# Moving the queries' relu from GpSimd to VectorE, and GpSimd's waits onto its edge columns

## The reference, cut to what matters

```python
x = x + window_mixing(group_norm(x))
x = x + linear_attention(group_norm(x))     # the second stage, below

qkv  = einsum('bchw,oc->bohw', x, w_qkv)            # 768 channels: queries, keys, values
y    = conv5x5_depthwise(qkv); y = conv1x1_grouped(y)
mqkv = concat([qkv, y], axis=1)                     # heads of 8 channels for each of q, k, v
q = relu(mqkv queries); k = relu(mqkv keys); v = mqkv values, with a row of ones
vk  = einsum('bhdn,bhen->bhde', v, k)
out = einsum('bhde,bhen->bhdn', vk, q)
out = out[:, :, :-1] / (out[:, :, -1:] + eps)
out = batch_norm(einsum('bchw,oc->bohw', out, w_proj))
```

## Time and profile before

| | |
|---|---|
| time, median of 3 runs | 2473.91 us (2470.03 to 2474.42) |
| profiled execution, span | 2473.8 us |
| busy in the span: PE, DVE, ACT, POOL | 95%, 81%, 60%, 44% |
| mean granted TensorE clock | 0.987 of full speed |
| DMA over the span | 628.38 MB, 254 GB/s |

### The profile page before, as it was taken

The page is one execution under the profiler, slowest core; times in us unless marked ns, Lnnn a source line. Parts: engine busy times, 40 slices in busy tenths (PEclk is TensorE's granted clock), DMA queues, the critical chain, the costliest instruction groups (busy, mean ns, idle before and its releaser), DMA issues. The chain is left out here.

```text
span 2473.8 us, 66794 instructions
## 1 busy us (share of the span) xinstructions
PE 2359.6 (95%) x25485; PEld 1881.3 (76%) x25485; DVE 1994.9 (81%) x2653; ACT 1495.6 (60%) x1864; POOL 1099.8 (44%) x1476
## 2 busy tenths in 40 slices
PE   5999799999999999799999999999999889999998
PEld 5889688877777887577888888888888656666666
DVE  7887688878788877778888888888888588888775
ACT  5777566666566666566776776677767434433442
POOL 7722387887787878200000000000000068888887
PEclk9999899999999999899999999999999999999999
DMA  7874689988988989988888888888888777777774
GB/s 285 336 301 173 208 295 344 329 293 314 316 288 323 344 299 302 253 196 207 209 209 208 209 210 207 210 208 209 207 208 210 228 243 280 275 275 271 271 272 136
DMA packets 300973, 628.38 MB, mean 254 GB/s; under 512 B 50784, under 2 KB 252256, under 8 KB 291552
## 3 DMA queue, kind: packets, MB, share of 16 engines
q1 hardware_dynamic: 295072, 590.38, 77.5%
q10 hardware_dynamic: 4688, 31.63, 3.6%
q0 software_dynamic: 1008, 3.67, 0.4%
HBM read 327.81 MB, written 300.94 MB: 254 GB/s over the span
## 5 line engine op out<-in xcount | busy, mean ns | idle before, releaser
L1562 PE MATMUL c_ps<-dh,wh 128*128 128x512 f32 x1152 | 465.3, 404 | 15.8 <-DVE wl L1712 9.9
L1477 ACT ACTIVATE dh<-image 128x1632 fp32r<-128x1632 f32 x192 | 301.5, 1570 | 269.9 <-PE c_ps L1562 254.8
L1562 PE MATMUL c_ps<-dh,wl 128*128 128x512 f32 x1152 | 456.4, 396 | 0.0
L1562 PE MATMUL c_ps<-dl,wh 128*128 128x512 f32 x1152 | 454.6, 395 | 1.6 <-issue 1.6
L1921 POOL TENSOR_TENSOR ql<-image,qh 128x1024 fp32r<-128x1024 f32 x1 | 2.4, 2359 | 967.8 <-DVE ql L2152 967.8
L1670 DVE TENSOR_TENSOR dl<-image,dh 128x1632 fp32r<-128x1632 f32 x192 | 356.3, 1856 | 73.9 <-ACT dh L1477 73.9
L1132 PE MATMUL o_ps<-xh,wqh 128*128 128x512 f32 x768 | 319.2, 416 | 11.3 <-issue 8.4
L1909 POOL TENSOR_TENSOR ql<-image,qh 128x1024 fp32r<-128x1024 f32 x126 | 300.9, 2413 | 10.7 <-ACT qh L1940 10.7
L1132 PE MATMUL o_ps<-xl,wqh 128*128 128x512 f32 x768 | 303.5, 395 | 0.0
L1132 PE MATMUL o_ps<-xh,wql 128*128 128x512 f32 x768 | 301.9, 393 | 0.0
L1562 PEld LDWEIGHTS c_ps<-dh,wh 128*128 128x128 f32 x1152 | 218.5, 190 | 68.6 <-DVE wl L1712 10.0
(11 more groups left out here) (212 smaller groups left out, 5107.8 us busy)
## 6 DMA issues: line engine op xcount, KB each, us to landing
qkv_scratch<-stage SPq DMA_DIRECT2D x384, 408.0 KB, 4.7
image<-qkv_scratch SPq DMA_DIRECT2D x189, 816.0 KB, 6.3
yq_scratch<-qy SPq DMA_DIRECT2D x64, 512.0 KB, 6.7
image<-qr_scratch SPq DMA_DIRECT2D x128, 256.0 KB, 6.1
image<-yq_scratch SPq DMA_DIRECT2D x128, 256.0 KB, 5.3
ox<-x_scratch SPq DMA_DIRECT2D x8, 4096.0 KB, 15.3
qr_scratch<-qs SPq DMA_DIRECT2D x126, 256.0 KB, 3.6
out<-ox SPq DMA_DIRECT2D x7, 4096.0 KB, 12.7
```

Of the source, the lines that this page charges most:

```text
L1477: act.activation(dh[kind][:, :], raw[kind], ACT.Copy).then_inc(hi_ready, 1)
L1562: last = pe.matmul(c_ps[:, m, :], w[hp][:, kind, part, o:o + P], cells[:, :, HALF * dy:HALF * dy + HALF * NB], start=(k == 0), stop=(k == 5))
```

## The change

The relu of the queries goes from GpSimd to VectorE, as one instruction of 128x1024 per chunk from `qw` to `qs`, behind VectorE's two differences of the queries. VectorE then also has the wait for the store of the `qs` buffer's former content. GpSimd's `pause` is gone, and its edge columns carry the waits; the edge columns become two-input instructions, with a tile of zeros as the other input (`0 - x` and `x + 0`). The border row is zeroed behind the first edge column of its chunk instead of ahead of it, and in those chunks the wait for the stored queries stands ahead of the keys' edge column.

```diff
+            pool.memset(zero[:, :], 0.0).then_inc(zeroed, 1)
             pool.memset(vT[:, :, :, :, SQ:VS], 1.0).then_inc(zeroed, 1)
+            pool.wait_ge(zeroed, 2)
+            none = zero[:, :].unsqueeze(1).unsqueeze(2).broadcast_to([P, 4, NB, 1])
...
-                    def pause(k, n):
-
-                        k = NCH * k + n
-                        pool.tensor_tensor(tick[:, k:k + 1], K["ident"][:, 0:1], K["ident"][:, 1:2], ALU.add)
-
                     def border(n):
 
                         row = NB * (1 - n // 4)
-                        keys_values_free(pool, b, n)
-                        queries_free(pool, b, n)
-                        pause(0, n)
...
                         if n % 2:
-                            pool.tensor_scalar(staged(j0, n, 0, 0, 1), every_second(buf, t0, n, 0, 1), -1.0, None, ALU.mult)
+                            pool.tensor_tensor(staged(j0, n, 0, 0, 1), none, every_second(buf, t0, n, 0, 1), ALU.subtract)
                         else:
-                            pool.tensor_copy(staged(j0, n, 1, HALF - 1, HALF), every_second(buf, t0, n, NB - 1, 1))
+                            pool.tensor_tensor(staged(j0, n, 1, HALF - 1, HALF), every_second(buf, t0, n, NB - 1, 1), none, ALU.add)
...
                         keys_values_free(pool, b, n)
-                        pause(1 + u, n)
+                        if u == 0 and n % 4 < 2:
+                            queries_free(pool, b, n)
                         edge(kv, 2 * u, 2 * u, n)
+                        if u == 0 and n % 4 < 2:
+                            border(n)
...
                         queries_free(pool, b, n)
-                        at_least(pool, K["qr_stored"][n % 2], 32 * (4 * b + n // 2))
-                        pause(3, n)
                         edge(qw, 0, 4, n)
                         pool.tensor_copy(staged(4, n, 2), every_second(qw, 0, n, 1 - n % 2)).then_inc(q_odd, 1)
-                        if end:
-                            return
-                        for t in range(2):
-                            last = pool.tensor_scalar(qs[:, n % 2, t, :], qw[:, n % 2, t, :], 0.0, None, ALU.max)
-                        last.then_inc(qs_ready, 1)
...
-                    def queries(n):
+                    def queries(n, end=False):
...
                         differences(qw, 0, 4, n, q_diff)
+                        if end:
+                            return
+                        at_least(dve, K["qr_stored"][n % 2], 32 * (4 * b + n // 2))
+                        dve.tensor_scalar(qs[:, n % 2, :, :], qw[:, n % 2, :, :], 0.0, None, ALU.max).then_inc(qs_ready, 1)
```

More of the change, by code:

```diff
@@ L767, in projections @@
         vT = sb("vT", [P, 2, 4, NSQ, VS])
-        tick = sb("ptick", [P, 4 * NCH])
+        zero = sb("zero", [P, 1])
         pw_rep = sb("pw_rep", [P, QT, NPH, D])
@@ L922, in keys_values, with queries @@
                         keys_values_free(pool, b, n)
-                        pause(1 + u, n)
+                        if u == 0 and n % 4 < 2:
+                            queries_free(pool, b, n)
                         edge(kv, 2 * u, 2 * u, n)
+                        if u == 0 and n % 4 < 2:
+                            border(n)
                         pool.tensor_copy(staged(2 * u, n, 2), every_second(kv, 2 * u, n, 1 - n % 2)).then_inc(kv_odd, 1)
-                    def queries(n, end=False):
+                    def queries(n):
                         g = NCH * b + n
@@ L931, in queries @@
                         queries_free(pool, b, n)
-                        at_least(pool, K["qr_stored"][n % 2], 32 * (4 * b + n // 2))
-                        pause(3, n)
                         edge(qw, 0, 4, n)
                         pool.tensor_copy(staged(4, n, 2), every_second(qw, 0, n, 1 - n % 2)).then_inc(q_odd, 1)
-                        if end:
-                            return
-                        for t in range(2):
-                            last = pool.tensor_scalar(qs[:, n % 2, t, :], qw[:, n % 2, t, :], 0.0, None, ALU.max)
-                        last.then_inc(qs_ready, 1)
                     for n in range(NCH):
-                        if n % 4 < 2:
-                            border(n)
                         keys_values(n, 0)
@@ L948, in body @@
                         keys_values(n, 1)
-                    queries(NCH - 1, last_body and par == 1)
+                    queries(NCH - 1)
             over_image_pairs(pool, body)
@@ L1107, in _ @@
                 last.then_inc(w_turned, 1)
-            pe.wait_ge(zeroed, 1)
+            pe.wait_ge(zeroed, 2)
             def product(b, n, j):
@@ L1324, in body @@
                             scale()
-                    queries(NCH - 1)
+                    queries(NCH - 1, not nxt)
                     dve.wait_ge(vk_full, NCH * (b + 1))
```

## The result

The changed kernel takes 2524.95 us (median of 4 runs, 2523.82 to 2525.92), the kernel before 2474.16 us (4 runs): a ratio of 1.0205, 95% interval 1.0192 to 1.0217. It is about 2% slower. Its profiled execution has a span of 2522.1 us, 48.3 us longer than that of before.

A forecast was written before the change was run, and what follows sets the result against it. TensorE's stream sets the time; X beyond its limits makes it wait. Terms of 20.9, 27.6 less about 1, 3, 1.2 and -4 give +48 us on 2473.8: 2522 us, 1.9% slower, range 2488 to 2547.

The forecast's parts named there:

- X: On VectorE, time from the start of value(n, 0) to that of value(n, 1); forecast to grow from 3.67 to 4.88 us.
- The limits of 3.97 and 3.77 us: Largest X before TensorE waits, in written-out images and in the loop; anything beyond passes one to one into the time.
- the 0.04 us beyond the wait: On TensorE, extra cost of about 0.04 us per late copy, as weights are then not preloaded.
- The relu's step: On VectorE inside X, time the 128x1024 relu adds: 0.68 us, extrapolated from 128x512 and 128x2 instructions.
- Contention: Inside X, GpSimd's edges (0.12 each) and copies (0.45 each) hold up VectorE: 1.1 us in place of 0.57.
- the fuller lock: Rival: each GpSimd instruction blocks VectorE for its full uncontended time, X 5.9, 2568 us; chance 0.09 together with a slow relu.
- The 22 written-out chunks: Images 0, 1, 6, 7, chunks 1 to 4, 6 and 7, less two: TensorE's waits add 20.9 us.
- The 24 of the loop: Loop chunks with the relu in X: 27.6 us, less about 1 that late chunks pay already.
- Chunk 5: Chunk where TensorE's weight load already waits for the norm's means: about 0.4 x 8 = 3 us.
- The last chunk: Chunk where TensorE already waits 1.65 us for VectorE's copy: +1.2 us.
- The 4 us taken off for chunks n = 1: In about five such chunks a DMA wait makes GpSimd fall behind and not contend: -0.8 x 5 = -4 us.
- Chunk 1 of image 0: Written-out chunk left out of the 22, as its delay was to disappear in the wait behind it.

The follow-up runs named there:

- e1: The changed kernel with the relu back on GpSimd, so only the pauses are gone: 2477.43 us, 1.0013 of the kernel before.
- e2: The kernel before with the relu on VectorE as in the change, GpSimd's pauses and one-input edges kept: 2492.62 us, 1.0075 of the kernel before.
- e3: The changed kernel with GpSimd's queries(n - 1) behind its keys_values(n, 1) instead of ahead of it: 2508.44 us, 1.0138 of the kernel before.
- e5: The changed kernel with the relu as two instructions of 128x512 in the same place: 2531.30 us, 1.0225 of the kernel before.
- e8: The kernel before with the relu on ScalarE ahead of the chunk's first copy of keys, pauses kept: 2475.64 us, 1.0010 of the kernel before.

## Why the prediction was right

Forecast 2522, measured 2524.95. The step that carries it, X, was forecast at 4.88 and is 4.90.

- **Where the room lies.** The limits of 3.97 and 3.77 us were read from one chunk each, with the 0.82 us of a chunk where the copy was late. They hold, and what goes beyond them passes one to one. Image 1, chunk 3 took 10.90 us before. It took 10.93 us in e1 (X = 3.84), 11.23 in e2 (4.25), 11.28 in e3 (4.30), 11.86 in the change (4.90) and 11.90 in e5 (4.94). The limit of 3.97 and the 0.04 us beyond the wait give 11.22, 11.27, 11.87 and 11.91 for the last four. In the loop, image 3, chunk 3 comes within 0.1 us of what the limit of 3.77 gives, in the same five kernels.
- **The relu's step:** 0.60 us, forecast 0.68 from the two short rows. The extrapolation was 0.08 too long. The formula that I had cited from the Trainium skill, "VectorE: DVE Perf Modes", section "The TRN2 errata", gave 0.6 us for the instruction; its uncontended duration here is 0.69 us.
- **Contention:** forecast 1.1, measured (0.76 - 0.61) + (1.07 - 0.61) + (0.67 - 0.55) + (1.07 - 0.60) = 1.2 us from the starts of an odd chunk (image 0, chunk 7). The order, edge against the second difference and so on down to copy against relu, is that of the timeline. e1 and e2 show each half without the other, and e3 shows that GpSimd's place makes the difference. The price of the fuller lock is refuted: a copy that takes 0.63 us beside PSUM work holds the next instruction up 0.46 us. The Trainium skill, "SBUF — State Buffer", section "SBUF: two separate sides", says that whichever starts first has the shared ports for its whole instruction and the other is fully blocked. The copy of 2.55 us is such a blocked one, but it was kept out by three VectorE instructions in a row, though it is recorded as starting ahead of all three.
- **Two misses that cancel.** The relu's step was forecast 0.08 too long and the contention, 0.12 + 0.45 + 0.12 + 0.45 = 1.14, came out 0.06 too short. That X is met within 0.02 us is partly luck.
- **The sum by its terms,** from the chunks' lengths in the two profiles. The 22 written-out chunks: 20 us (20.9 forecast). The 24 of the loop: 27 (26.6). Chunk 5: 4.7 (3). The last chunk: 1.3 (1.2). These are right but for chunk 5.
- **What was wrong.** The 4 us taken off for chunks n = 1, where a DMA wait would keep GpSimd out of X, did not come: X is 4.90 or 4.91 in all eight. Chunk 1 of image 0 did not lose its 0.95 us to the wait behind it either. And chunks n = 0 were not unchanged: 0.2 us each in the loop, as the relu of chunk 7 comes ahead of the sums of the image. So the projections grew by 55.5 us between the first and the last `sum_vk`, some 8 more than the sum, and their start by another 1.8. The 300 us that GpSimd's busy time was to fall by were 230, since what it still does got longer.
- **What offset it.** From the last `sum_vk` to the end the profile after is 9.0 us shorter. 1.5 us of this is a shorter handover to the convolutions (8.6 in place of 10.1 us). The other 7.4 lie behind their first matmul, where nothing was changed. In the profiles of e1 to e8 that stretch takes 1454 to 1460 us, in the change 1456, in the profile of before 1463.4; so I take it for scatter between executions, which no run shows directly. Without it the projections alone would have made 57 us of the span, 9 more than forecast. That the total came out 3 us from the median owes something to luck. The medians, 50.8 us apart, lie between the two.

## What to carry to other kernels

Room is a place, not a sum: 123 us of waiting on VectorE did not cover 63 relus of 0.69 us (1.08 us with their contention), as they stood behind the wait, on the way from one of TensorE's products to its next transposes. With the same instructions further down VectorE's stream the loss was 8 us in place of 51. And an instruction that seems to do nothing may set when an engine meets another: before taking it out, write down, for each instruction of the two engines, which one runs beside which, before and after.

## What the hardware showed that I had not expected

GpSimd's wide copy and VectorE's SBUF instructions delay each other by amounts that hang on which of them gets in first. A copy that began beside a VectorE instruction held up the next by 0.46 us and took 1.06. One in image 0, chunk 4 took 2.55 us and held up nothing, and six others that began at the same distance to VectorE's instructions did not fare so. A one-source relu of 128x1024 is held up like a two-source difference (0.47 and 0.46 us), and the 128x1024 subtraction of `split` likewise: beside GpSimd's copy its step in image 0, chunk 6 is 1.61 us, beside GpSimd's relu before it was 1.14, and its mean is 1663 ns after against 1276 before.
